# A Swin block on one core: plain float32 products in 128x32 tiles, a fourth strip of tokens moved by DMA, against split products

## The chip, the cores and the metric

The kernel runs on one core of one Trainium2 chip. The metric is the device time of one execution in microseconds (us).

## What is computed

The input x is float32 of shape (4, 96, 128, 128): 4 images, 96 channels. One Swin transformer block is followed by a generalised divisive normalisation. Cut to what matters:

```python
y = ln(x, norm1) ; roll by (-4, -4) ; cut into 8x8 windows of N = 64 tokens
qkv = y @ qkv_w.T + qkv_b              # 6 heads of 16 channels
attn = softmax(q @ k.T * 16 ** -0.5 + mask)
out = (attn @ v) @ proj_w.T + proj_b   # windows put back, rolled by (4, 4)
x2 = x + out
h1 = gelu(ln(x2, norm2) @ w1.T + b1)   # 384 hidden channels
x3 = x2 + h1 @ w2.T + b2
result = x3 * rsqrt(gamma @ x3**2 + beta)   # over the 96 channels
```

## The kernel before, in words

**Halves and rounds.** A unit is one row of 16 windows (1024 tokens); there are 64 units, and each is worked in two halves of 512 tokens, so 128 halves. The program is a software pipeline: in round H each engine runs its stages, every stage on half H plus its offset. The offsets stand in one line of constants: TURN_IN 4, TURN_OUT 3, QK 1, ATTEND 0, PROJECT -1, MLP -2, SETTLE -3, DIVIDE -4. The order in which an engine takes its stages is written out by hand in a function `steps`, one for each engine, and every engine works strictly in that order. In the last rounds a hand-written list (`late`) takes the place of the loop.

**Layouts.** Products have channels on 96 partitions and 512 tokens in the free dimension. The sums of probabilities and the product with v (lines 1081 to 1094) already use tiles of 128 rows and 32 columns of the array: three head pairs go to partitions 0 to 95, for 384 tokens each, and the fourth strip of partitions (96 to 127) takes the other 128 tokens of all three, so that four tiles work together. The division (lines 831 and 833) brings that strip back to the three head pairs in three short instructions.

**Products in parts.** q, k, the way up and down of the MLP and the denominators run as three float32r products each (`in_parts`, line 999: high times high, low times high, high times low). The parts of the activations are made by GpSimd (`split_hi`, `split_lo`, lines 452 and 457), those of the MLP's input y2 by VectorE (`split_y2`). The projection (line 1105) is one plain float32 product. v (line 1032) is 32 small plain products.

**Keys.** k goes from PSUM to SBUF by ScalarE (`k_copy`, line 577), and SyncE's queue (SP) then copies it by six DMAs, one for each head, into the block-diagonal `k_block` (`copy_keys`, line 378). `scores` (line 1058) waits for them. SP also loads x (two DMAs for a unit, line 350) and stores the output (two DMAs for a unit, line 387). SP issues in order: a DMA whose wait is not met holds back those behind it.

**Banks.** Two PSUM banks serve nearly all products in turn (`MM_ITEMS`); a product waits until the product two places before it has been read out. ScalarE loads a table twice a round (line 539), once for gelu and once for exp and ln.

## Time and profile before

| | |
|---|---|
| median of 3 runs | 1768.49 us (1768.0 to 1774.17) |
| span of the profiled execution | 1766.9 us |
| around the span: median less span | 1.6 us |
| busy: TensorE, VectorE, ScalarE, GpSimd | 97%, 92%, 86%, 77% |
| chain that ended last | 96% on TensorE |
| DMA | mean 46 GB/s, 81.35 MB |

The times shown are those of whole executions; the span is from the first to the last instruction of one profiled execution, whose own time is not listed apart. Busy shares are of the span. Register, semaphore and DMA-issuing instructions are not counted as busy, so SyncE has no share there; its issues are seen in the timeline and by line.

### The profile page before, as it was taken

Reading aid. Unit: us, or ns where it says so; the run is one execution under the profiler, and the core shown is the slowest. Engines: PE = TensorE matmul, PEld = TensorE weight load, DVE = VectorE, ACT = ScalarE, POOL = GpSimd, SP = SyncE. Lnnn points to the kernel's source line nnn. Section 1 sums busy time; section 2 is a strip of 40 time slices with the busy share of each in tenths; the row PEclk is TensorE's granted clock in tenths of the full one; section 3 lists DMA queues with packets and bytes.
Section 4 is the critical chain, followed back from the end, with each engine's and each line's share of the span. In section 5 each row is a group of like instructions: output and inputs, shape, how many; then the busy total and the mean of one; then the engine's idle time right before and its main releaser. Section 6 shows DMA issues by size and latency. Waiting matters only on the chain.

```text
span 1766.9 us, 81406 instructions
## 1 busy us (share of the span) xinstructions
PE 1720.2 (97%) x32612; PEld 1252.8 (71%) x32612; DVE 1629.6 (92%) x4508; ACT 1527.5 (86%) x2832; POOL 1356.5 (77%) x1532
## 2 busy tenths in 40 slices
PE   4999999999999999999999999999999999999996
PEld 2677777777777777777777777777777777777763
DVE  5899999999999999999999999999999999999983
ACT  2798998988898988988898888998888898998986
POOL 3478878878878878878778877888878878878862
PEclk9999999999999999999999999999999999999997
DMA  2122122122122122122122122122122122122111
GB/s 58 27 46 52 37 54 52 37 54 53 37 53 52 36 54 52 38 53 52 36 55 52 36 55 50 37 56 52 35 56 49 37 56 51 37 55 52 28 32 27
DMA packets 215154, 81.35 MB, mean 46 GB/s; under 512 B 116118, under 2 KB 214780, under 8 KB 214780
## 3 DMA queue, kind: packets, MB, share of 16 engines
q1 hardware_dynamic: 214218, 76.04, 19.7%
q8 instruction: 261, 4.28, 1.0%
q14 instruction: 113, 0.93, 0.2%
q10 hardware_dynamic: 562, 0.11, 0.0%
HBM read 25.75 MB, written 25.17 MB: 29 GB/s over the span
## 4 chain that ended last, share of the span: by engine, by line
PE 96%; DVE 1%; issue 1%; ACT 1%; DMA 0%; SPq 0%; POOL 0%; POOLq 0%; DVEq 0%
PE mm_bank L999 49%; PE score_banks L1058 8%; PE score_banks L947 7%; PE mm_bank L1105 6%; PE mm_bank L1032 5%; PE pv_bank L1081 5%; PE turn_banks L939 5%; PE turn_banks L953 3%; PE mm_bank L1094 3%; PE mm_bank L1091 3%; PE score_banks L1066 1%; PE mm_bank L1134 0%; DMA x_ext<-in_x 0%; DVE stats L767 0%; SPq L378 0%
## 5 line engine op out<-in xcount | busy, mean ns | idle before, releaser
L457 POOL TENSOR_TENSOR hidden_lo<-hidden,hidden_hi 128x512 fp32r<-128x512 f32 x378 | 480.9, 1286 | 0.0
L618 ACT ACTIVATE hidden<-mm_bank 128x512 f32<-128x512 f32 x381 | 227.8, 598 | 124.1 <-PE mm_bank L999 111.8
L539 ACT ACT_TABLE_LOAD x253 | 324.6, 1283 | 4.5
L452 POOL TENSOR_SCALAR y_hi<-y 96x512 fp32r<-96x512 f32 x128 | 108.1, 845 | 206.8 <-ACT y L563 206.8
L812 DVE TENSOR_REDUCE row_max<-score_banks 128x8 f32<-128x512 f32 x384 | 250.8, 681 | 10.8 <-PE score_banks L1066 8.1
L820 DVE TENSOR_TENSOR shifted<-score_banks,row_max 128x512 f32<-128x512 f32 x384 | 250.7, 680 | 0.0
L469 POOL TENSOR_TENSOR x_sq<-x 96x512 f32<-96x512 f32 x126 | 130.8, 1038 | 152.2 <-DVE x L846 152.2
L585 ACT ACTIVATE probs<-shifted 128x512 f32<-128x512 f32 x384 | 236.2, 627 | 10.6 <-DVE shifted L820 3.4
L452 POOL TENSOR_SCALAR hidden_hi<-hidden 128x512 fp32r<-128x512 f32 x378 | 229.8, 619 | 1.3 <-ACT hidden L618 1.3
L597 ACT ACTIVATE probs_t<-score_banks 128x512 f32<-128x512 f32 x384 | 215.1, 602 | 0.0
L767 DVE BATCH_NORM_STATS2 stats<-turn_banks 128x6 f32<-128x96 f32 x1024 | 191.1, 248 | 17.1 <-PE turn_banks L939 17.1
L947 PEld LDWEIGHTS score_banks<-ident_sb,probs 64*128 64x128 f32 x3072 | 148.3, 139 | 53.9 <-ACT probs L585 28.2
L947 PE MATMUL score_banks<-ident_sb,probs 64*128 64x64 f32 x3072 | 184.3, 230 | 1.6 <-issue 1.1
L999 PE MATMUL mm_bank<-y_hi,w_hi 97*128 97x512 f32 x381 | 172.1, 452 | 1.0 <-ACT hidden L618 0.6
L457 POOL TENSOR_TENSOR y_lo<-y,y_hi 96x512 fp32r<-96x512 f32 x128 | 164.3, 1284 | 1.1 <-POOL y_hi L452 1.1
L457 POOL TENSOR_TENSOR x_sq_lo<-x_sq,x_sq_hi 96x512 fp32r<-96x512 f32 x126 | 160.9, 1277 | 0.7 <-POOL x_sq_hi L452 0.7
L999 PE MATMUL mm_bank<-hidden_hi,w_hi 128*96 128x512 f32 x378 | 160.6, 425 | 0.0
L776 DVE TENSOR_TENSOR turn_banks<-turn_banks,moments 128x384 f32<-128x384 f32 x256 | 145.0, 567 | 8.8
L1058 PE MATMUL score_banks<-k_block,q 32*64 32x128 f32 x6144 | 148.6, 275 | 3.9 <-DMA k_block<-k 2.5
L999 PE MATMUL mm_bank<-y_lo,w_hi 97*128 97x512 f32 x381 | 151.4, 397 | 0.0
L999 PE MATMUL mm_bank<-y_hi,w_lo 97*128 97x512 f32 x381 | 150.5, 395 | 0.0
L999 PE MATMUL mm_bank<-hidden_hi,w_lo 128*96 128x512 f32 x378 | 149.7, 396 | 0.0
(132 smaller groups left out, 4489.2 us busy)
## 6 DMA issues: line engine op xcount, KB each, us to landing
x_ext<-in_x SPq DMA_DIRECT2D x128, 192.0 KB, 2.9
k_block<-k SPq DMA_DIRECT2D x768, 32.0 KB
out<-o_ext SPq DMA_DIRECT2D x128, 192.0 KB, 2.6
w_raw<-in_w_t SPq DMA_DIRECT2D x1, 144.0 KB
w<-in_w_t SPq DMA_DIRECT2D x1, 144.0 KB
qkv_raw<-in_qkv_t ACTq DMA_DIRECT2D x1, 108.0 KB
ident_sb<-in_ident SPq DMA_DIRECT2D x1, 64.0 KB, 2.2
q_quadrants<-in_qmask SPq DMA_DIRECT2D x3, 1.0 KB
```

Source lines behind the costliest of these rows:

```text
L452: nc.gpsimd.tensor_scalar(hi, whole, 1.0, 1.0, ALU.mult, ALU.mult).then_inc(hi_ready, 1)
L457: nc.gpsimd.tensor_tensor(lo, whole, hi, ALU.subtract).then_inc(is_split, 1)
L539: nc.scalar.preload_act_table_set(name)
L585: nc.scalar.activation(probs[:, g, :, :, :].rearrange("t p j k -> t (p j k)"), shifted[:, g, :, :].rearrange("t i k -> t (i k)"), ACT.Exp)\
L597: nc.scalar.activation(dst, src, ACT.Copy).then_inc(probs_t_ready, 1)
L618: nc.scalar.activation(hidden_of(A)[:, n, :], up_bank(A, n), ACT.Gelu).then_inc(gelu_ready, 1)
L767: made = nc.vector.bn_stats(stats[ln][:, c, :], turn_banks[:, ln, n * DIM:(n + 1) * DIM])
L812: nc.vector.tensor_reduce(row_max[:, g, :], group_scores(g), op=ALU.max, axis=AX.X)\
L820: nc.vector.tensor_tensor(shifted[:, g, :, :], group_scores(g), row_max[:, g, :].unsqueeze(2) .broadcast_to([128, PAIRS * TILE_HEADS, TOKE ...
L947: return nc.tensor.transpose(score_banks[:, bank, first:first + TOKENS], probs[half, m, p, :, :], ident_sb[half, half])
L999: made = nc.tensor.matmul(out, w, x_part, start=first and part == 0, stop=last and part == 2)
L1058: made = nc.tensor.matmul(score_banks[64 * n:64 * n + 64, r, cols], q[rows, unit_slot(a), (w + n) * TOKENS:(w + n + 1) * TOKENS], k_block[ ...
```

## The change

- q, k, the projection, the way down and the denominators become plain float32 products in 128x32 tiles (`in_strips`): three matmuls of 384 tokens for the three groups of 32 output channels, and three of 128 tokens whose results all go to the fourth strip. The way up stays in three float32r parts. v becomes four matmuls with all 128 columns for the tokens of a pair of windows, written to `pv_bank` (no `mm_bank`); `v_blocks` then makes four copies in place of one masked product.
- In that layout q, attended, x2 and x3 hold the last (or first) 128 tokens on partitions 96 to 127. The residuals (`first_residual`, `second_residual`) and `outputs` work on 128 partitions and 384 columns. x is loaded with the strip beside it (five DMAs for a unit in place of two), and the output is stored by five. Where a product contracts over the channels, the strip has to come back to partitions 0 to 95: SP does this with three DMAs for q, three for attended and three for x3, for each half. The keys go in 12 DMAs (six windows from partitions 0 to 95, two from the strip, for each head) in place of six.
- GpSimd no longer splits anything. It squares x3 and adds the biases of the projection and of the MLP to x and x2 (`bias_x`, `bias_x2`). The projection and MLP biases leave the matrices.
- The mean of the layer norms is taken out through the weights (their column sums, at the start), so the centring of the tokens and the aggregation instructions go, and four small VectorE instructions a round (`variances`) give the variance.
- The pipeline is deeper: PROJECT -2, MLP -3 (now only the turning of y2), UP -4 (the way up), SETTLE -5, DIVIDE -6. The hand-written end goes; the loop runs on for seven rounds. q comes right after k; the projection and the way down come ahead of the transposes of probabilities; v, now behind them.

The core of the diff (the renaming of arguments and the declarations are left out):

```diff
-X_SLOTS = 4
+X_SLOTS = 5
+Y_SLOTS = 3
+X2_SLOTS = 4
+KEY_COPIES = 2 * HEADS
+IMAGE_MOVES = 5
 QKV_CONSTS = 6
-MLP_CONSTS = 9
-MLP_WEIGHTS = 3
-
-TURN_IN, TURN_OUT, QK, ATTEND, PROJECT, MLP, SETTLE, DIVIDE = 4, 3, 1, 0, -1, -2, -3, -4
+MLP_CONSTS = 19
+FOLDS = 17
+
+TURN_IN, TURN_OUT, QK, ATTEND, PROJECT, MLP, UP, SETTLE, DIVIDE = 4, 3, 1, 0, -2, -3, -4, -5, -6
 
...
         MM_ITEMS = [
             ("k", QK, k_ready, 1, 1),
+            ("q", QK, q_ready, 1, 1),
             ("den", DIVIDE, log_den_made, 1, 1),
             ("sum", ATTEND - 1, log_sum_made, 1, 1),
-            ("v", ATTEND, v_ready, 1, 1),
-            ("q", QK, q_ready, 1, 1),
+            ("proj", PROJECT, x2_ready, 1, 1),
             ("mlp2", SETTLE, x3_ready, 1, 1),
-            ("proj", PROJECT, x2_ready, 1, 1),
-            ("mlp1_0", MLP, gelu_ready, HID_CHUNKS, 1),
-            ("mlp1_1", MLP, gelu_ready, HID_CHUNKS, 2),
-            ("mlp1_2", MLP, gelu_ready, HID_CHUNKS, 3),
+            ("mlp1_0", UP, gelu_ready, HID_CHUNKS, 1),
+            ("mlp1_1", UP, gelu_ready, HID_CHUNKS, 2),
+            ("mlp1_2", UP, gelu_ready, HID_CHUNKS, 3),
         ]
-        FINAL = HALVES - 1
-        MM_FINISH = [
-            ("sum", FINAL), ("den", FINAL - 3), ("proj", FINAL), ("mlp2", FINAL - 2),
-            ("mlp1_0", FINAL - 1), ("mlp1_1", FINAL - 1), ("mlp1_2", FINAL - 1), ("den", FINAL - 2),
-            ("mlp2", FINAL - 1), ("mlp2", FINAL), ("den", FINAL - 1), ("den", FINAL),
-        ]
-        MM_ORDER = [(item[0], H + item[1]) for H in range(-TURN_IN - 1, HALVES) for item in MM_ITEMS
-                    if has(H + item[1])] + MM_FINISH
+        MM_ORDER = [(item[0], H + item[1]) for H in range(FIRST_ROUND, END_ROUND) for item in MM_ITEMS
+                    if has(H + item[1])]
...
+            def load_x(A):
...
+                    first = image_rows(unit)[0][1]
+                    for j in range(HEAD_PAIRS):
+                        sp.dma_start(x_ext[strip, slot, 2 + 2 * j:4 + 2 * j, 0:WIDTH],
+                                     x[bass.ds(unit // ROWS, 1), group(j), bass.ds(first, 2), :]
+                                     .rearrange("n c h w -> (n c) h w")).then_inc(x_loaded[slot], 16)
...
+            def copy_keys(A):
 
...
+                first, last = (A % 2) * HALF_WINDOWS, (A % 2 + 1) * HALF_WINDOWS
                 for head in range(HEADS):
                     rows = slice(HEAD_DIM * head, HEAD_DIM * (head + 1))
...
-                    sp.dma_start(k_block[rows, half_windows(a), head % TILE_HEADS, :],
-                                 half_of(k, a)[rows, :].rearrange("c (n t) -> c n t", t=TOKENS))\
-                        .then_inc(keys_copied[a % 2], 16)
...
+                    sp.dma_start(k_block[rows, first:last - 2, head % TILE_HEADS, :],
+                                 k[rows, A % 2, :].rearrange("c (n t) -> c n t", t=TOKENS))\
+                        .then_inc(keys_copied[A % 2], 16)
+                for head in range(HEADS):
+                    rows = slice(HEAD_DIM * head, HEAD_DIM * (head + 1))
+                    at = DIM + HEAD_DIM * (head % TILE_HEADS)
+                    sp.dma_start(k_block[rows, last - 2:last, head % TILE_HEADS, :],
+                                 k[at:at + HEAD_DIM, A % 2, group(head // TILE_HEADS, 128)]
+                                 .rearrange("c (n t) -> c n t", t=TOKENS)).then_inc(keys_copied[A % 2], 16)
+
+            def move_queries(A):
+
+                wait_alone(sp, q_ready, A + 1)
+                for j in range(HEAD_PAIRS):
+                    sp.dma_start(q[group(j), A % 2, MAIN:HALF], q[strip, A % 2, group(j, 128)])\
+                        .then_inc(q_moved[A % 2], 16)
+
+            def move_attended(A):
+
+                wait_alone(sp, attended_ready, A + 1)
+                for j in range(HEAD_PAIRS):
+                    sp.dma_start(attended[group(j), MAIN:HALF], attended[strip, group(j, 128)])\
+                        .then_inc(attended_moved, 16)
+
+            def move_x3(A):
+
+                wait_alone(sp, x3_ready, A + 1)
+                for j in range(HEAD_PAIRS):
+                    sp.dma_start(x3[group(j), A % 2, MAIN:HALF], x3[strip, A % 2, group(j, 128)])\
+                        .then_inc(x3_moved[A % 2], 16)
+
...
+                    stores = [(to[:, bass.ds(first + 2, 2), :], o_ext[0:DIM, slot, 2:4, 0:WIDTH]),
+                              (to[:, bass.ds(second, SHIFT), :], o_ext[0:DIM, slot, 4:8, 0:WIDTH])]
+                    stores += [(to[group(j), bass.ds(first, 2), :],
+                                o_ext[strip, slot, 2 + 2 * j:4 + 2 * j, 0:WIDTH]) for j in range(HEAD_PAIRS)]
+                    for dst, src in stores:
+                        sp.dma_start(dst, src).then_inc(out_stored[slot], 16)
...
-                run(store_out, DIVIDE - 1)
+                run(move_queries, QK)
+                run(move_attended, ATTEND - 1)
+                run(move_x3, SETTLE)
+                run(store_out, DIVIDE)
...
+            def bias_x(A):
+
+                if A % 2 == 1:
+                    if A == 1:
+                        wait_alone(pool, mlp_loaded, 16 * MLP_CONSTS)
+                    wait_alone(pool, x_turned[0], A + 1)
+                    rows = x_ext[:, unit_slot(A, X_SLOTS), 2:WIN, :].rearrange("c (j i) w -> c j (i w)", i=2)
+                    width = 2 * (WIDTH + SHIFT)
+                    nc.gpsimd.tensor_tensor(rows, rows, proj_bias[:, :].unsqueeze(2)
+                                            .broadcast_to([128, HEAD_PAIRS, width]), ALU.add).then_inc(x_biased, 2)
+
+            def bias_x2(A):
+
+                wait_alone(pool, x_turned[1], A + 1)
+                tokens = by_group(x2[:, A % X2_SLOTS, :])
+                nc.gpsimd.tensor_tensor(tokens, tokens, b2_bias[:, :].unsqueeze(2)
+                                        .broadcast_to([128, HEAD_PAIRS, 128]), ALU.add).then_inc(x2_biased, 1)
+
...
+            def divide(A):
                 dve.wait_ge(inv_sum_ready, A + 1)
                 dve.wait_ge(pv_made, A + 1)
                 wait(dve, proj_made, A)
-                for m in range(HEAD_PAIRS):
-                    cols = slice(m * 2 * TOKENS, (m + 1) * 2 * TOKENS)
-                    nc.vector.tensor_tensor(attended[32 * m:32 * m + 32, MAIN:HALF], pv_bank[DIM:128, cols],
-                                            inv_sum[DIM:128, cols], ALU.mult)
-                nc.vector.tensor_tensor(attended[0:DIM, 0:MAIN], pv_bank[0:DIM, 0:MAIN],
-                                        inv_sum[0:DIM, :], ALU.mult).then_inc(attended_ready, 1)
-
-            def first_residual(A, a):
+                nc.vector.tensor_tensor(attended[:, 0:MAIN], pv_bank[:, 0:MAIN], inv_sum[:, :],
...
+            def in_strips(to, weights, main, last):
+
+                for j in range(HEAD_PAIRS):
+                    nc.tensor.matmul(to[group(j), 0:MAIN], weights[:, group(j)], main, start=True, stop=True)
+                for j in range(HEAD_PAIRS):
+                    made = nc.tensor.matmul(to[strip, group(j, 128)], weights[:, group(j)], last,
+                                            start=True, stop=True)
+                return made
+
...
+            def project_v(A):
+
+                wait(pe, attended_ready, A)
+                for p in range(PAIRS):
+                    made = nc.tensor.matmul(pv_bank[:, p * DIM:(p + 1) * DIM], y1_windows(A, 2 * p, 2 * p + 2),
+                                            wv[:, :], start=True, stop=True)
                 made.then_inc(v_made, 1)
...
+                pe.wait_ge(gelu_ready, HID_CHUNKS * (A + 1))
                 mm_wait("mlp2", A)
+                to = mm_bank("mlp2", A)
                 for n in range(HID_CHUNKS):
-                    pe.wait_ge(gelu_ready, HID_CHUNKS * A + n + 1)
-                    made = nc.tensor.matmul(mm_bank("mlp2", A)[0:DIM, :], w2[:, n, :], hidden_of(A)[:, n, :],
-                                            start=n == 0, stop=n == HID_CHUNKS - 1)
+                    first, last = n == 0, n == HID_CHUNKS - 1
+                    for j in range(HEAD_PAIRS):
+                        nc.tensor.matmul(to[group(j), 0:MAIN], w2[:, n, group(j)], hidden[:, n, 128:HALF],
+                                         start=first, stop=last)
+                    for c in range(HID_CHUNKS):
+                        made = nc.tensor.matmul(to[strip, group(n, 128)], w2[:, c, group(n)],
+                                                hidden[:, c, 0:128], start=c == 0, stop=c == HID_CHUNKS - 1)
                 made.then_inc(mlp2_made, 1)
...
-            def denominators(A, a):
-                pe.wait_ge(sq_split, A + 1)
-                mm_wait("den", A)
-                in_parts(mm_bank("den", A)[0:DIM, :], wgdn_hi[:, :], wgdn_lo[:, :],
-                         x3_sq_hi[:, :], x3_sq_lo[:, :]).then_inc(den_made, 1)
+                in_strips(mm_bank("den", A), wgdn, x3_sq[:, 0:MAIN], x3_sq[:, MAIN:HALF]).then_inc(den_made, 1)
 
             def steps(run, H):
 
                 run(scores, ATTEND)
                 run(project_k, QK)
+                run(project_q, QK)
                 run(denominators, DIVIDE)
                 run(sum_probs, ATTEND - 1)
                 run(times_v, ATTEND - 1)
+                run(project, PROJECT)
+                run(mlp_down, SETTLE)
+                turn_run(H)
                 run(project_v, ATTEND)
-                run(project_q, QK)
-                turn_run(H)
-                for n in range(HID_CHUNKS):
-                    run(mlp_down, SETTLE, n)
-                run(project, PROJECT)
+                run(mlp_up, UP, 0)
                 run(turn_in, TURN_IN, 0)
                 if H == -TURN_IN:
```

On SP two rounds in the middle of the program, of before. The rows give the line of the kernel, the destination and source and the destination's shape:

```order
L350 DMA x_ext<-in_x 96x4x128 [waits x2_ready]
L350 DMA x_ext<-in_x 96x4x128
L378 DMA k_block<-k 16x8x64 [waits k_ready,scores_made]
L378 DMA k_block<-k 16x8x64 x5
L378 DMA k_block<-k 16x8x64 [waits k_ready,scores_made]
L378 DMA k_block<-k 16x8x64 x5
L387 DMA out<-o_ext 96x4x128 [waits out_wrapped]
L387 DMA out<-o_ext 96x4x128
```

And one round of the change, the one with a store, with the start of the next:

```order
L362 DMA k_block<-k 16x6x64 [waits k_ready,scores_made]
L362 DMA k_block<-k 16x6x64 x5
L368 DMA k_block<-k 16x2x64 x6
L376 DMA q<-q 32x128 [waits q_ready]
L376 DMA q<-q 32x128 x2
L383 DMA attended<-attended 32x128 [waits attended_ready]
L383 DMA attended<-attended 32x128 x2
L390 DMA x<-x 32x128 [waits x3_ready]
L390 DMA x<-x 32x128 x2
L404 DMA out<-o_ext 96x2x128 [waits out_wrapped]
L404 DMA out<-o_ext 96x4x128
L404 DMA out<-o_ext 32x2x128 x3
```

In two rounds SP has 16 DMAs before and 52 now; a round always holds 21, and a load or a store of five comes in every second one each.

On TensorE, from the scores to the transposes of the probabilities, of before:

```order
L1058 MATMUL score_banks<-k_block,q 64x128 x24
L1066 MATMUL score_banks<-k_masks,q_quadrants 64x128 x3
L999 MATMUL mm_bank<-y_hi,wk_hi 96x512
L999 MATMUL mm_bank<-y_hi,wk_lo 96x512
L999 MATMUL mm_bank<-y_lo,wk_hi 96x512
L999 MATMUL mm_bank<-x_sq_hi,wgdn_hi 96x512
L999 MATMUL mm_bank<-x_sq_hi,wgdn_lo 96x512
L999 MATMUL mm_bank<-x_sq_lo,wgdn_hi 96x512
L1091 MATMUL mm_bank<-probs_t,ones_pair_sb 32x384 x3
L1094 MATMUL mm_bank<-probs_t,ones_pair_sb 32x128 x3
L1081 MATMUL pv_bank<-probs_t,v_block 32x64 x24
L1032 MATMUL mm_bank<-wv,y 32x48 x32
```

And of the change:

```order
L1030 MATMUL score_banks<-k_block,q 64x128 x24
L903 MATMUL mm_bank<-y,wk 32x384 x3
L905 MATMUL mm_bank<-y,wk 32x128 x3
L903 MATMUL mm_bank<-y,wq 32x384 x3
L905 MATMUL mm_bank<-y,wq 32x128 x3
L903 MATMUL mm_bank<-x_sq,wgdn 32x384 x3
L905 MATMUL mm_bank<-x_sq,wgdn 32x128 x3
L1062 MATMUL mm_bank<-probs_t,ones_pair_sb 32x384 x3
L1065 MATMUL mm_bank<-probs_t,ones_pair_sb 32x128 x3
L1051 MATMUL pv_bank<-probs_t,v_block 32x64 x24
L903 MATMUL mm_bank<-attended,wproj 32x384 x3
L905 MATMUL mm_bank<-attended,wproj 32x128 x3
```

q has moved ahead of the denominators, and from k to the way down everything is one shape of tile.

## Rows read from the trace of the kernel before

**Rows 1.** The page, parts 1 and 4: TensorE's busy time; the chain by engine.

```profile
PE 1720.2 (97%) x32612; PEld 1252.8 (71%) x32612; DVE 1629.6 (92%) x4508; ACT 1527.5 (86%) x2832; POOL 1356.5 (77%) x1532
...
PE 96%; DVE 1%; issue 1%; ACT 1%; DMA 0%; SPq 0%; POOL 0%; POOLq 0%; DVEq 0%
```

**Rows 2.** The waits of SP's queue: waited for, us in total, times, longest.

```profile
SPq L241 <- ACT k L577: 799.4, 128, 15.6
SPq L241 <- DVE x L838: 150.9, 60, 5.2
SPq L241 <- POOL o_ext L498: 59.3, 22, 24.7
```

**Rows 3.** SP's issues by line: duration ns min/median/max, first and last start us.

```profile
L378 SPq DMA_DIRECT2D k_block<-k x768: 585/601/1867, 26.7 to 1706.7; - x192
...
L350 SPq DMA_DIRECT2D x_ext<-in_x x128: 319/474/1903, 1.2 to 1631.3; - x128
```

**Rows 4.** Timeline of SP, first 12 us: start us, us, line, out<-in xcount.

```profile
3.06 0.32 SPq L402 DMA_DIRECT2D gdn_raw<-in_gamma_t  x1
...
5.01 0.42 SPq L402 DMA_DIRECT2D ones_pair_sb<-in_ones_pair  x1
5.48 0.43 SPq L402 DMA_DIRECT2D wproj<-in_proj_t  x1
```

**Rows 5.** Timeline of SP, 803 to 817 us, in short windows.

```profile
803.11 0.60 SPq L378 DMA_DIRECT2D k_block<-k  x1
...
803.84 2.25 SPq L387 DMA_DIRECT2D out<-o_ext  x2
...
812.45 1.24 SPq L378 DMA_DIRECT2D k_block<-k  x2
...
813.73 1.37 SPq L378 DMA_DIRECT2D k_block<-k  x1
...
816.43 0.60 SPq L378 DMA_DIRECT2D k_block<-k  x1
```

**Rows 6.** The page, part 6: a DMA's median time from issue to landing, last.

```profile
x_ext<-in_x SPq DMA_DIRECT2D x128, 192.0 KB, 2.9
```

**Rows 7.** Timeline of TensorE, one round: start us, us until the last ends.

```profile
803.50 0.48 PE L999 MATMUL mm_bank<-hidden_hi,w_hi 128*96 128x512 f32 x1
...
805.67 1.02 PE L1105 MATMUL mm_bank<-attended,wproj 97*96 97x512 f32 x2
806.53 0.50 PE L939 MATMUL turn_banks<-ident_sb,x_ext 96*128 96x96 f32 x4
...
810.70 0.47 PE L999 MATMUL mm_bank<-y_hi,wk_hi 97*96 97x512 f32 x1
...
811.49 0.39 PE L999 MATMUL mm_bank<-x_sq_hi,wgdn_hi 97*96 97x512 f32 x1
...
812.34 0.52 PE L1091 MATMUL mm_bank<-probs_t,ones_pair_sb 128*32 128x384 f32 x3
...
813.01 0.86 PE L1081 MATMUL pv_bank<-probs_t,v_block 128*32 128x64 f32 x48
813.68 0.88 PE L1032 MATMUL mm_bank<-wv,y 97*32 97x48 f32 x64
814.48 0.48 PE L999 MATMUL mm_bank<-y_hi,wq_hi 97*96 97x512 f32 x1
```

**Rows 8.** Timeline of ScalarE around the exponential table's load.

```profile
808.86 1.28 ACT L618 ACTIVATE hidden<-mm_bank 128x512 f32<-128x512 f32 x2
810.16 1.28 ACT L539 ACT_TABLE_LOAD   x1
811.69 0.59 ACT L577 ACTIVATE k<-mm_bank 96x512 f32<-96x512 f32 x1 [0.25 <-PE mm_bank L999]
```

**Rows 9.** The last stretch: us, PE, PEld, DVE, ACT, POOL busy, PEclk, DMA share, GB/s.

```profile
1740.00:1767.00 27.00, 16.21 (x51) 8.54 (x50) 9.13 (x20) 11.97 (x18) 3.80 (x5) 0.82 0.11 29
```

**Rows 10.** Groups of VectorE's instructions by line: busy us, mean ns, idle before.

```profile
L776 DVE TENSOR_TENSOR turn_banks<-turn_banks,moments 128x384 f32<-128x384 f32 x256 | 145.0, 567 | 8.8
```

778 lines of the change are left out of this document (334 added, 444 removed).

## The prediction

> **What bounds the kernel now.** I read the page first: TensorE is busy for 1720.2 of 1766.9 us and the chain that ended last lies on it for 96% [rows 1]. So today a round lasts as long as TensorE's work in it. The first key copy is issued at 26.7 us and the last at 1706.7 [rows 3]; 127 rounds lie between, 13.2 us each. Ahead of them are 27 us, behind them 60.
>
> The change takes work from TensorE, VectorE and GpSimd and adds DMAs, all on SP. So the next view is the one on SP's queue. It waits 799.4 us for k, 150.9 us for x2 and 59.3 us for the output, 1010 us in all [rows 2]. The other 757 us are issuing: 5.9 us a round for 8 DMAs. The reader is to see in [rows 3, 5] that an issue isn't free: a key copy holds SP for at least 585 ns and 601 at the median; two follow each other 0.64 us apart; and six of them, 812.45 to 817.03, take 4.58 us because one took 1.37. The order of SP before and after says what is added: 52 DMAs in two rounds in place of 16, 18 more a round.
>
> **The change on SP.** What does an added issue cost? The trace shows three kinds.
> - The second six key copies have the kind of the first (SBUF to SBUF, 16 partitions, windows apart): 0.64 us each, 3.8 a round [rows 5].
> - The nine moves of strips (32 partitions, 512 bytes each, SBUF to SBUF) have no row of their own. By shape they are nearest to the weight loads, which follow each other 0.47 us apart (5.01 to 5.48) [rows 4]; by place, both ends in SBUF, to the key copies at 0.64. I take the middle, 0.56: 5.0 a round. The ends kept for the range are 0.36 (the shortest load, 319 ns [rows 3], with a gap of 0.04) and 0.76 (the mean in the burst with the long issue).
> - Three more loads or stores a round, the loads' median 474 ns [rows 3], with the gap 0.52: 1.6.
> - Three more waits on semaphores: after the last key copy (803.11 plus 0.60) the store is issued 0.13 later, 0.09 more than between two copies [rows 5]: 0.3 a round.
>
> Sum: 5.9 + 3.8 + 5.0 + 1.6 + 0.3 = **16.6 us a round on SP**, against 13.2 for a whole round today. The cover is gone: SP had 7.3 us idle a round, and 10.7 are added. Put the other way, the round stays at 13.2 only if the 18 added issues cost (13.2 - 5.9 - 0.3) / 18 = 0.39 us each; every row that follows another issue is above that, only issues after an idle queue are below. With all 18 at 0.36 SP needs 12.7, with 15 at 0.47 it is 14.8, with 15 at 0.76 it is 19.2.
>
> Does SP really work without a break then? The waits in front of it: with q of the next half issued at time T, its landing is about 2 us later (a DMA takes 2.9 from issue to landing, issue included [rows 6]), scores 0.94, k 0.67, its copy 0.6: k of the half after is ready at T + 4.3. SP meanwhile issues attended, x3 and on average 5 loads and stores, 6.2 us. attended and x3 belong to halves whose products began a round before. So every wait of SP is met when it comes to it, and its sum is the round.
>
> **The change on the engines**, hidden by that. TensorE: between the rows of one round [rows 7] k takes 0.79 us, the denominators 0.85, the way down 2.17, the projection 0.86, v 0.80, and the sums of probabilities, the very form that the change gives to all, 0.67. q, k, denominators and projection at 0.67 and the way down at 3 x 0.65 save 0.12 + 0.15 + 0.18 + 0.19 + 0.22 = 0.86. v as four matmuls lies between 0.28 (four transposes of 96 columns, 806.53 to the next product) and 0.80; I take 0.70. So 13.26 becomes about 12.3 and, masks counted only every second round, 12.1. But the order has a new wait: the denominators use the bank of k and the sums that of q. k can be copied only behind two gelus and the table load [rows 8], and q behind k and the two short rstd instructions, about 3.5 us after the scores' start, when TensorE would be at the sums after 2.95. That gives back 0.5 or more: **12.8**.
> VectorE loses the centring (145.0 us [rows 10]), the aggregation, the three short divisions and a fourth of the residuals' and outputs' columns, and gains four small instructions and copies of v in place of a product: well under its 1630 us [rows 1], no bound. ScalarE keeps both table loads and drops a quarter of the columns of k, q and the denominators: less than its 1528, so below 11.9 a round. GpSimd loses all splitting, most of its 1357 us, and gains two additions. All this lies beside SP's queue and is worth nothing while that decides.
>
> At 812.34 the sums begin 0.15 later than the preceding products' pace would let them [rows 7], at a change of tile shape. The Trainium skill ("TensorEngine Tiling (Array Packing)", Key Properties) says that changing the tiling mode drains the engine; the new order has two such changes fewer a round, so by it TensorE would need some 0.2 us less, which moves the engines' 12.8 and not SP's 16.6.
>
> **Sum.** 27 us to the first key copy, 127 rounds of 16.6 (2108), less 12 because the first six rounds have no x3 to move, and an end of 65: seven rounds run on, one full at 12.8, the others with little but the MLP, two table loads of 1.28 and three gelus, near 7 each; today's hand-made end takes 60. 27 + 2108 - 12 + 65 = 2188 in the profile's time; the median of runs is 1.6 above the span shown, so **2190 us**.
>
> **Rivals.**
> 1. *SP's issues are cheap and the engines decide: faster.* If a two-dimensional or small copy holds SP for no more than 0.32 to 0.33 us, as the shortest load does [rows 3], SP's sum falls to 12.7 and the round is the 12.8 of the engines: 27 + 127 x 12.8 + 65 = 1718, **1720 us**. The point from which it decides is 0.37 us an added issue. For it: the spare time on all engines, and a weight load of 0.32 [rows 4]. Against it: 768 key copies with none below 585 ns. The Trainium skill ("SBUF — State Buffer", The DMA setup-cost knee) makes nearly all of a DMA's fixed 2 us completion latency and puts sequencer and generator at about 50 ns plus a few hundred. At 250 ns, an estimate from that page, SP would need 10.7 us a round and this rival would hold; the key copies' rows do not agree with it.
> 2. *The loop through the keys.* Moves cheap, keys not: then SP's sum can fall below the loop from scores to the next scores: 0.94 + 0.67 + 0.6 for k, 12 keys of 0.64 (7.7), the wait and two issues of q (1.2), 2.9 from the last issue to landing: 14.0. 27 + 127 x 14.0 + 55 is about **1860 us**. For it speaks that scores now wait for q's move, issued behind twelve keys; it decides once SP's sum is below 14.0.
> 3. *The clock falls.* TensorE would be idle 4 us in each round, ahead of the scores. In the last 27 us, where it is busy for 16.21, its granted clock is 0.82, a mixture of 2.4 and 1.2 GHz [rows 9]. A third of each round at 1.2 GHz would fit in the 16.6; the whole of it would be about 24 us a round and over 3000 us. Its price starts only beyond the idle time.
>
> **How the numbers follow.** SP's queue as the bound has 0.71, the loop 0.09, the clock 0.04, the engines 0.16. The first three are slower; of the last I give 0.02 to an outcome near 1768, where the added issues are about 0.39. A measurement tells about 0.5% from no change. So faster 0.14, same 0.03, slower 0.83. The range takes in the loop and, of SP's sums, 13.9 to 18.6 us a round: 1840 to 2440 us. It leaves out the engines' case and 0.04 above.
>
> **What would show it.** In the profile after: SP waiting for almost nothing; key copies still near 600 ns, moves 0.45 to 0.6; TensorE near 70 to 75% busy, its idle time ahead of the scores and ended by the moves of q or the keys; the products in tiles 0.67 us apart; VectorE under 1500 us busy; a round of 16 to 17 us. I'm wrong if moves of strips issue in 0.35 us or less, if SP still waits hundreds of us for k, or if TensorE's longest idle time is ended by ScalarE's copies.

## The result, and the profile after

The change takes **2375.59 us** (median of 4 runs, 2366.15 to 2380.48) against 1771.33 us for the kernel before on the same chip: ratio 1.3403, 95% interval 1.3365 to 1.3442. The profiled execution has a span of 2375.1 us and a mean granted clock of 0.875 on TensorE.

The page of the kernel after, parts 1, 2 (TensorE's clock) and 4, beside [rows 1]:

```profile
PE 1927.0 (81%) x33524; PEld 1643.2 (69%) x33524; DVE 1397.8 (59%) x3886; ACT 1473.8 (62%) x2829; POOL 355.6 (15%) x459
...
PEclk9799889989889888888898888889898898889888
...
SPq 86%; issue 8%; PE 3%; DMA 1%; ACT 0%; DVE 0%; POOL 0%; POOLq 0%; DVEq 0%
SPq L362 22%; SPq L368 22%; SPq L390 11%; SPq L376 9%; SPq L383 9%; SPq L404 6%; SPq L334 4%; SPq L329 3%; PE mm_bank L905 1%; PE score_banks L1030 1%; DMA q<-q 1%; SPq L238 1%; DMA x<-x 1%; PE mm_bank L1101 0%; PE mm_bank L903 0%
```

The chain that ended last lay on TensorE for 96%; now it lies on SP's queue for 86%, and the key copies (L362, L368) and the moves of strips (L376, L383, L390) are its largest parts. No engine is busy for more than 81%.

The waits of SP's queue after, for which [rows 2] stand before:

```profile
SPq L238 <- ACT k L565: 25.8, 9, 5.7
SPq L238 <- DVE x L825: 24.7, 4, 8.5
SPq L238 <- DVE attended L809: 12.6, 2, 8.3
SPq L238 <- POOL o_ext L493: 6.2, 1, 6.2
```

1010 us of waiting have become 69, and of these only 2.4 lie between 200 and 2290 us: there SP issues without a break.

SP's issues by line after (duration ns min/median/max, first and last start us), for [rows 3]:

```profile
L362 SPq DMA_DIRECT2D k_block<-k x768: 589/602/1991, 24.6 to 2292.8; - x192
...
L368 SPq DMA_DIRECT2D k_block<-k x768: 585/593/1831, 28.6 to 2297.1; - x192
...
L376 SPq DMA_DIRECT2D q<-q x384: 542/590/1753, 32.5 to 2299.0; - x192
...
L383 SPq DMA_DIRECT2D attended<-attended x384: 507/590/1921, 66.7 to 2324.8; - x192
...
L390 SPq DMA_DIRECT2D x<-x x384: 507/590/1934, 134.1 to 2364.1; - x192
...
L404 SPq DMA_DIRECT2D out<-o_ext x320: 322/451/2093, 170.6 to 2372.8; - x160
```

The moves have their own rows now: 590 ns at the median, as dear as the key copies, though each of them moves one piece of 512 bytes a partition. An issue with an end in DRAM (L404) takes 451. From L362's first start to its last, 127 rounds take 2268.2 us: **17.86 us a round**, where [rows 3] gave 13.2.

One round of SP's timeline after (start us, us, line, count), and the moves of q and x3 of the next, for [rows 5]:

```profile
1144.01 3.88 SPq L362 DMA_DIRECT2D k_block<-k  x6
1147.94 4.32 SPq L368 DMA_DIRECT2D k_block<-k  x6
1152.38 1.83 SPq L376 DMA_DIRECT2D q<-q  x3
1154.33 1.79 SPq L383 DMA_DIRECT2D attended<-attended  x3
1156.23 1.78 SPq L390 DMA_DIRECT2D x<-x  x3
1158.13 1.03 SPq L329 DMA_DIRECT2D x_ext<-in_x  x2
1159.21 2.38 SPq L334 DMA_DIRECT2D x_ext<-in_x  x3
...
1170.60 1.83 SPq L376 DMA_DIRECT2D q<-q  x3
...
1174.43 2.72 SPq L390 DMA_DIRECT2D x<-x  x3
```

The next round begins at 1161.77. Nothing lies between the issues of two lines but 0.05 to 0.18 us. Six copies take 3.88, or 4.32 where one of them is long; the nine moves with their waits take 5.75 (1152.38 to 1158.13); the three loads of L334 take 2.38, and if two of them took the median of 0.43, one took 1.44.

The scores shown next wait for the moves of q issued from 1170.60 on, the denominators behind them for the moves of x3 issued from 1174.43 on. TensorE's timeline after, 1173 to 1180 us, for [rows 7]:

```profile
1173.92 1.85 PE L1030 MATMUL score_banks<-k_block,q 32*64 32x128 f32 x48 [2.01 <-DMA q<-q]
1175.71 0.86 PE L903 MATMUL mm_bank<-y,wk 97*32 97x384 f32 x3
...
1176.99 0.86 PE L903 MATMUL mm_bank<-y,wq 97*32 97x384 f32 x3
...
1179.72 0.86 PE L903 MATMUL mm_bank<-x_sq,wgdn 97*32 97x384 f32 x3 [1.23 <-POOL x_sq L485]
```

and its waits over the whole span (us in total, times, longest), with GpSimd's own wait behind the first of them:

```profile
POOL x_sq L485 <- DMA x<-x: 1478.2, 128, 24.5
...
PE mm_bank L903 <- POOL x_sq L485: 270.3, 119, 5.1
PE score_banks L1030 <- DMA q<-q: 114.4, 62, 8.1
```

TensorE waits in two places: ahead of the scores for q's moves, in 62 rounds, and longer ahead of the denominators, in 119 rounds, for the squares, which GpSimd can make only when the moves of x3, the last of SP's moves in a round, have landed. Both waits end with SP's queue.

The clock. The windows of the round from 1160 us (us, PE, PEld, DVE, ACT, POOL busy, PEclk, DMA share, GB/s):

```profile
1160.00:1172.00 12.00, 11.56 (x207) 9.82 (x199) 9.66 (x25) 9.54 (x21) 1.52 (x3) 1.00 0.23 52
1172.00:1177.50 5.50, 3.58 (x66) 3.02 (x70) 2.62 (x10) 2.01 (x3) 0.00 (x0) 0.70 0.10 25
```

TensorE was idle for 2.01 us up to 1173.92, and the second window, which holds that idle time, has a granted clock of 0.70, a mixture of the two levels (2.4 and 1.2 GHz). k takes 1.28 here (1175.71 to 1176.99) and the scores 1.79; in a round at the full clock (from 1210 us) they take 0.67 and 1.05. That lies beside SP's issuing; b_more18 below shows how far the clock is a consequence.

### The profile page after: what moved, and what is told of

It reads as the page before. It is cut to its first block, busy times and chain, and to the rows that moved or that the text cites. A ratio compares the mean times of both kernels' runs of the same rounds, so it can differ in the third digit from the quotient of the medians.

```text
span 2375.1 us, 84051 instructions
## 1 busy us (share of the span) xinstructions
PE 1927.0 (81%) x33524; PEld 1643.2 (69%) x33524; DVE 1397.8 (59%) x3886; ACT 1473.8 (62%) x2829; POOL 355.6 (15%) x459
## 4 chain that ended last, share of the span: by engine, by line
SPq 86%; issue 8%; PE 3%; DMA 1%; ACT 0%; DVE 0%; POOL 0%; POOLq 0%; DVEq 0%
SPq L362 22%; SPq L368 22%; SPq L390 11%; SPq L376 9%; SPq L383 9%; SPq L404 6%; SPq L334 4%; SPq L329 3%; PE mm_bank L905 1%; PE score_banks L1030 1%; DMA q<-q 1%; SPq L238 1%; DMA x<-x 1%; PE mm_bank L1101 0%; PE mm_bank L903 0%
## 5 line engine op out<-in xcount | busy, mean ns | idle before, releaser
L903 PE MATMUL mm_bank<-x_sq,wgdn 97*32 97x384 f32 x768 | 158.3, 706 | 270.8 <-POOL x_sq L485 270.3
L816 DVE TENSOR_TENSOR x<-mm_bank,x_ext 128x384 f32<-128x384 f32 x128 | 71.3, 557 | 420.5 <-PE mm_bank L905 420.5
L1101 PE MATMUL mm_bank<-hidden,w 128*32 128x128 f32 x2304 | 286.9, 281 | 0.0
L1098 PE MATMUL mm_bank<-hidden,w 128*32 128x384 f32 x2304 | 285.3, 507 | 0.1
L1101 PEld LDWEIGHTS mm_bank<-hidden,w 128*32 128x32 f32 x2304 | 263.5, 115 | 5.1
L1030 PE MATMUL score_banks<-k_block,q 32*64 32x128 f32 x6144 | 168.5, 300 | 115.9 <-DMA q<-q 114.4
L1030 PEld LDWEIGHTS score_banks<-k_block,q 32*64 32x64 f32 x6144 | 132.4, 146 | 164.3 <-issue 164.3
L771 DVE TENSOR_TENSOR y_lo<-turn_banks,y_hi 96x512 fp32r<-96x512 f32 x128 | 87.9, 687 | 194.2 <-ACT y L547 191.2
L553 ACT ACTIVATE y_hi<-turn_banks 96x512 fp32r<-96x512 f32 x128 | 76.0, 593 | 202.7 <-PE turn_banks L941 202.7
L784 DVE COPY v_block<-pv_bank 64x192 f32<-64x192 f32 x512 | 180.6, 353 | 12.3 <-PE pv_bank L1005 7.1
L1051 PEld LDWEIGHTS pv_bank<-probs_t,v_block 128*32 128x32 f32 x6144 | 180.8, 155 | 5.7
```

What stands on the lines that cost most here:

```text
L1030: made = nc.tensor.matmul(score_banks[64 * n:64 * n + 64, r, cols], q[rows, A % 2, (2 * p + n) * TOKENS:(2 * p + n + 1) * TOKENS], k_block ...
L1098: nc.tensor.matmul(to[group(j), 0:MAIN], w2[:, n, group(j)], hidden[:, n, 128:HALF], start=first, stop=last)
L1101: made = nc.tensor.matmul(to[strip, group(n, 128)], w2[:, c, group(n)], hidden[:, c, 0:128], start=c == 0, stop=c == HID_CHUNKS - 1)
```

## The experiments

A round is here the time from the first to the last matmul of the scores, divided by 127. The third column is the kernel before on the same chip in the same series. Where "one run" stands, the kernel ran once, and there is no interval.

| kernel | us | before | ratio, 95% interval | round, us |
|---|---|---|---|---|
| before | 1771.33 | | | 13.2 |
| after | 2375.59 | 1771.33 | 1.3403 (1.3365 to 1.3442) | 17.9 |
| b_more9 | 1783.79 | 1769.02 | one run | 13.4 |
| b_more18 | 2415.09 | 1769.02 | one run | 18.3 |
| a_noq | 2142.76 | 1769.02 | one run | 16.0 |
| a_pool | 1878.42 | 1769.02 | 1.0603 (1.0552 to 1.0653) | 13.9 |
| b_tiny18 | 2153.97 | 1774.70 | one run | 16.3 |
| a_tiny3 | 2609.25 | 1774.70 | one run | 19.7 |
| a_nomoves | 1802.59 | 1774.70 | 1.0171 (1.0138 to 1.0203) | 13.5 |
| a_pool2 | 1857.36 | 1774.70 | 1.0489 (1.0447 to 1.0532) | 13.8 |
| b_load18 | 1769.35 | 1773.85 | one run | 13.2 |
| a_nomoves_up | 1762.36 | 1773.85 | 0.9951 (0.9928 to 0.9975) | 13.2 |
| a_pool3 | 1860.74 | 1773.85 | 1.0520 (1.0470 to 1.0571) | 13.8 |
| a_pool4 | 1822.73 | 1769.43 | 1.0291 (1.0266 to 1.0317) | 13.5 |

**b_more9 and b_more18: the kernel before, with SP's added issues alone.** Nothing of the change is in them but 9 or 18 more DMAs a round on SP, each of 16 KB between two SBUF tiles. The edit is shown with 18; b_more9 has 9 in its place.

```diff
+            def spare_moves(A, a):
+                if A > 1:
+                    wait_alone(sp, spare_moved[A % 2], 16 * 18 * (A // 2))
...
+                for n in range(18):
+                    sp.dma_start(spare[32 * (n % 3):32 * (n % 3) + 32, A % 2, n // 3, :], ident_sb[96:128, :])\
+                        .then_inc(spare_moved[A % 2], 16)
...
                 run(copy_keys, QK)
+                run(spare_moves, QK)
```

> The kernel before, with nine more copies a round on SP (32 partitions of 512 bytes, from the identity matrix to a spare tile; the result does not use them). Theory (SP's issues set the change's round): SP then needs 5.9 + 9 x 0.66 + 0.1 = 11.9 us a round, under the 13.2 of TensorE, so the time stays within 1% of 1770 us. Rival (more DMAs slow the others by traffic or by landing later): slower by several per cent already here.

> The kernel before, with eighteen more such copies a round, as many DMAs as the change adds, and nothing else of the change. Theory: SP needs 5.9 + 18 x 0.66 + 0.1 = 17.9 us a round, above 13.2, so 127 x 17.9 + 90 = 2360 us, the change's own time. Rival (the new products, their new waits for ScalarE and the fallen clock make the change slow): about 1770 us, or a small loss.

With nine, 1783.79 us: SP still waits 185 us, and the round is nearly unchanged. With eighteen, 2415.09 us, 40 us more than the change itself and 55 more than expected: 227 of the 2304 added issues took over 0.9 us, and their mean was 0.67. SP's waits in b_more18:

```profile
SPq L243 <- POOL o_ext L513: 35.4, 3, 23.7
SPq L243 <- ACT k L592: 15.7, 1, 15.7
```

Between nine and eighteen SP's idle time of 7.3 us a round is used up, and from there each issue lengthens the round. The clock comes out at 0.864 in b_more18, where TensorE's products are those of the kernel before: so the low clock needs nothing of the new tiles; that TensorE is made to wait is enough.

**a_noq: the change with three of the moves fewer.** The part of q that they would bring is zero, so these scores are left out.

```diff
-                run(move_queries, QK)
...
-                wait_alone(pe, q_moved[A % 2], 16 * HEAD_PAIRS * (A // 2 + 1))
```

> The change without the three moves of q a round; that part of q is set to zero once, so the scores of the last two windows of each half are left out of the computation. Theory: three issues of 0.66 us and a wait of 0.1 go from SP's round of 17.9: 15.8, 2375 - 128 x 2.1 = 2107 us. Rival (engines or clock set the round): within 2% of 2375 us. Rival (the landing of q ahead of the scores is what costs, 114 us of TensorE's waits): 2260 us.

2142.76 us, 36 above what was expected and far from both rivals. Three issues and a wait less are 233 us less, 1.83 a round, 0.61 for each, which is what the three take in SP's timeline (1.83). So these issues were on the path with their whole length. With them gone SP's queue is still 68% of the chain and waits 85 us.

**a_tiny3: the change with three more DMAs of 4 bytes.** The edit is `spare_moves` with 3 and the shape of b_tiny18 below.

> The change with three more DMAs a round on SP, each of 4 bytes in one partition. Theory: with SP full, even tiny issues lengthen the round: 3 x 0.34 + 0.1 = 1.1 us, 2375 + 128 x 1.1 = 2516 us. Rival (bytes, landings or engines set the round): within 1% of 2375 us.

2609.25 us, 234 more for 384 DMAs of 4 bytes, 0.61 each. The expectation was 93 too low: it counted on issues 0.34 apart, and these took 598 ns at the median. The mean clock falls further, to 0.829.

**b_tiny18 and b_load18: what makes an issue dear.** First the 18 added DMAs with 4 bytes in place of 16 KB, both ends in SBUF:

```diff
+                    sp.dma_start(spare[n:n + 1, A % 2, 0, 0:1], ident_sb[96:97, 0:1])\
```

> The kernel before with eighteen more DMAs a round on SP, each of 4 bytes in one partition. Theory (the time that an issue holds SP is what counts): an issue of one partition took 0.25 to 0.33 us at the start, so SP needs 5.9 + 18 x 0.34 + 0.1 = 12.1 us a round, under 13.2: 1770 to 1800 us. Rival (the number of DMAs or of their landings counts, whatever their size): about 2400 us, as with the eighteen larger copies.

2153.97 us, neither the one nor the other. Size matters little between SBUF and SBUF: an issue took 543 ns with 4 bytes here, and 598 in a_tiny3, where those of the moves take 590. What the small ones lack is long issues: none of the 2304 took over 0.70 us. So the next run kept the 4 bytes and changed where they come from, DRAM instead of SBUF:

```diff
-                    sp.dma_start(spare[n:n + 1, A % 2, 0, 0:1], ident_sb[96:97, 0:1])\
+                    sp.dma_start(spare[n:n + 1, A % 2, 0, 0:1], ident[96:97, 0:1])\
```

> The kernel before with 18 more DMAs of 4 bytes a round on SP, as in b_tiny18, but each with its source in DRAM (a constant of the inputs) in place of SBUF. Theory (an issue is dear when both ends are in SBUF, whatever its size): with a DRAM end an issue takes 0.28 to 0.33 us (the shortest load of the kernel before takes 319 ns), apart 0.33; SP needs 5.9 + 0.1 + 18 x 0.33 = 11.9 us a round, below 13.2, so the time stays within 1.5% of the kernel before (1775 to 1800). Rival (every further issue costs near 0.59, whatever its ends, because SP issues faster than the rings drain): 16.5 us a round again and about 2150 us.

1769.35 us, level with the kernel before. The 18 issues by line (duration ns min/median/max) and in SP's timeline (start us, us), first of b_tiny18:

```profile
L391 SPq DMA_DIRECT2D spare<-ident_sb x2304: 542/543/697, 30.6 to 2105.4; - x192
```
```profile
1004.66 10.68 SPq L391 DMA_DIRECT2D spare<-ident_sb  x18
```

and the same two views of b_load18:

```profile
L391 SPq DMA_DIRECT2D spare<-in_ident x2304: 220/252/448, 30.7 to 1712.2; - x192
```
```profile
1005.47 5.73 SPq L391 DMA_DIRECT2D spare<-in_ident  x18
```

The same 4 bytes cost SP 0.59 us an issue from SBUF to SBUF and 0.32 from DRAM to SBUF. The number of DMAs and of landings is the same in both, so they are not what costs. For 4 bytes the source decides the price. For larger DMAs with an end in DRAM it doesn't alone: the loads and stores of this kernel take 427 to 510 ns at the median. The moves of this change have the dear kind. The Trainium skill ("SBUF — State Buffer", The DMA setup-cost knee) puts sequencer and generator at about 50 ns and a few hundred: the row of b_load18, 252 ns, agrees; that of b_tiny18, 543, is about twice the row of b_load18. Why, no run here tells.

**a_nomoves: what would be left if SP had nothing to move.** The nine moves and the waits for them are gone, and what they would bring of q, attended and x3 is a constant, so these tokens are left out. SP keeps the keys, the loads and the stores.

```diff
-                run(move_queries, QK)
-                run(move_attended, ATTEND - 1)
-                run(move_x3, SETTLE)
...
-                wait_alone(pe, q_moved[A % 2], 16 * HEAD_PAIRS * (A // 2 + 1))
...
-                pe.wait_ge(attended_moved, 16 * HEAD_PAIRS * (A + 1))
...
-                wait_alone(pool, x3_moved[A % 2], 16 * HEAD_PAIRS * (A // 2 + 1))
```

> The change without any of the nine moves and without the waits for them; the strips' last columns of q, attended and x3 are constants, so these tokens are left out of the computation. It measures the engines' round of the change. Forecast of the prediction: 12.8 us a round, 1720 us. Rival (the engines have not gained, 13.2 us a round or more, because v in four matmuls takes 0.9 us and the way up now waits for y2's low part, both seen in the run with moves on GpSimd): 1770 to 1800 us. Rival (the landing of moves played no part and the clock or TensorE itself is the bound): above 1850 us.

1802.59 us, 1.7% above the kernel before. Even with SP out of the way the engines' side of the change is not faster. TensorE's timeline of a_nomoves shows a place where it stands:

```profile
1000.91 1.13 PE L1005 MATMUL pv_bank<-wv,y 97*128 97x96 f32 x8
1001.83 0.47 PE L1085 MATMUL mm_bank<-y_hi,w_hi 97*128 97x512 f32 x1
...
1003.06 0.52 PE L922 MATMUL turn_banks<-ident_sb,x_ext 96*128 96x96 f32 x4 [0.30 <-DVE y_lo L771]
```

v takes 0.92 us (1000.91 to 1001.83), against 0.80 for the 32 small matmuls in [rows 7]. Ahead of the turning of x TensorE waits for y2's low part to be read out of the bank, 121 times, 35.8 us in all. And from the second half of q to the denominators it is 0.60 (1007.66 to 1008.26), where half a product takes 0.32. By the order of the banks this is the wait for the one that k's copy frees; no row names it.

**a_nomoves_up: that wait covered.** a_nomoves, and on TensorE:

```diff
                 run(mlp_up, UP, 0)
+                run(mlp_up, UP, 1)
                 run(turn_in, TURN_IN, 0)
...
                 run(turn_in, PROJECT, 1)
-                run(mlp_up, UP, 1)
                 run(mlp_up, UP, 2)
```

> a_nomoves (the change without its nine moves, so its output lacks what the moved strips carry) with the second chunk of the way up moved ahead of the turning of x. Theory (TensorE waits 0.3 us a round for y2's low part ahead of the turning, and this is what keeps the engines' round of the change at 13.47): the 0.7 us of the way up cover that wait, the round falls to 13.2 and the time from 1803 to about 1770, level with the kernel before. Rival (the wait only moves, to the scores, that wait for the keys 0.3 us later anyway, or to the third chunk that waits for its bank): 1795 to 1805.

1762.36 us (8 runs, 1757.2 to 1770.98), 0.5% below the kernel before and 40 us below a_nomoves. The wait is gone from TensorE's timeline:

```profile
1010.28 0.39 PE L1085 MATMUL mm_bank<-y_lo,w_hi 97*128 97x512 f32 x1
1010.51 0.49 PE L922 MATMUL turn_banks<-ident_sb,x_ext 96*128 96x96 f32 x4
```

This is the best that the engines' side of the change gave in these runs, the moves left out: a round of 13.17 in place of 13.24. It isn't quite the engines alone: SP's queue, with 12 key copies a round, is 17% of the chain, and TensorE waits 31.3 us, in 35 rounds, for key copies.

**a_pool, a_pool2, a_pool3, a_pool4: the whole change, its moves issued elsewhere.** GpSimd is idle for 85% of the change, so in a_pool it issues the nine moves:

```diff
-                run(move_queries, QK)
-                run(move_attended, ATTEND - 1)
-                run(move_x3, SETTLE)
                 run(store_out, DIVIDE)
...
+                run(move_queries, QK)
                 run(wrap_out, DIVIDE)
+                run(move_attended, ATTEND - 1)
+                run(move_x3, SETTLE)
                 run(square, SETTLE)
```

> The change with the nine moves of q, attended and x3 issued by GpSimd, which is busy 15% of the time, in place of SP. Theory: SP is left with 12 keys and 5 loads and stores, 11.7 us a round, so the engines' round decides: 12.8 us forecast, 1720 us, if GpSimd can issue nine DMAs in under 9 us. Rival (the DMAs themselves, their landing or the engines are the bound): within 3% of 2375 us. Between them if GpSimd needs over a microsecond for each issue: its 2.8 us of work and 9 issues then are the round.

1878.42 us. Most of the loss is back, 497 of 604 us, by moving nine issues from one queue to another. An issue costs GpSimd 498 ns at the median. The rest of the expected gain was held by waits that the expectation hadn't counted: TensorE's waits in a_pool (us in total, times, longest),

```profile
PE turn_banks L922 <- DVE y_lo L771: 35.6, 121, 1.0
PE mm_bank L903 <- POOL x_sq L461: 32.3, 20, 5.2
PE mm_bank L1062 <- ACT q L559: 26.5, 16, 2.0
PE score_banks L1030 <- DMA k_block<-k: 25.6, 18, 5.9
```

and behind the second of them GpSimd's square, which waits 258.7 us for the moves of x3 just ahead of it in its own queue. a_pool2 puts the moves of x3 first and q's copy ahead of the rstd instructions:

```diff
                 run(move_queries, QK)
-                run(wrap_out, DIVIDE)
-                run(move_attended, ATTEND - 1)
                 run(move_x3, SETTLE)
+                run(move_attended, ATTEND - 1)
                 run(square, SETTLE)
+                run(wrap_out, DIVIDE)
...
-                rstd_pair(H)
                 run(q_copy, QK)
+                rstd_pair(H)
```

> The change with the nine moves on GpSimd as before, there x3's moves first and the output's wrap behind the square, and on ScalarE the copy of q ahead of the two rstd instructions. In the run with moves on GpSimd TensorE waited 77 us for the squares and 27 us and more for the copy of q. If these waits are what the round has over the engines' own, 1878 - 100 = 1780 us; if the engines alone set it, still 1850 or more.

1857.36 us: 21 us better, 77 above what was expected. The expectation had added TensorE's wait for the squares (32.3 us) and that of its weight loads (45.1 us), which lie beside each other. The scores' wait for the keys had grown to 36.9 us. a_pool3 is a_pool2 with the reordering of a_nomoves_up:

> a_pool2 (the whole change, with its nine moves issued by GpSimd, nothing left out) with the same reordering as a_nomoves_up. Theory: 0.3 us a round less, 1857 falls to about 1820, still above the kernel before, since the keys' 12 issues on SP stay on the loop from k to the scores. Rival: if that loop decides in most rounds, nothing is gained, 1850 to 1860. If everything the engines can give shows, 1770.

1860.74 us, the rival's case: what the reordering had given a_nomoves (40 us) shows nowhere here. TensorE's wait ahead of the scores in a_pool3:

```profile
PE score_banks L1030 <- DMA k_block<-k: 63.2, 70, 4.7
```

Each time one wait went, the keys' wait grew: 25.6, 36.9, 63.2 us. The edit of a_pool2 has a part in that. With the output's wrap behind the square, SP now waits for the wrap at every store, and the keys of the next half stand behind the store. SP's waits and timeline in a_pool3:

```profile
SPq L238 <- POOL o_ext L490: 185.8, 64, 18.5
```
```profile
1000.51 3.12 SPq L383 DMA_DIRECT2D out<-o_ext  x5
1003.82 3.80 SPq L362 DMA_DIRECT2D k_block<-k  x6
```

k was copied out at 1002.72 there, 1.1 us before its first copy was issued. In a_pool SP waited for the wrap 5 times, 65.4 us, and for k in all 128 rounds; in a_pool3 it waits for k in 73. Over the rounds 8 to 119 of a_pool3, the scores wait 31 us for keys issued behind a store and 12 us for those behind a load. The order without this wait (moves of x3 first, the wrap where it was) was not run.

a_pool4 takes six of the twelve key copies off SP and puts them on GpSimd behind q's moves:

```diff
-                for head in range(HEADS):
...
-                    sp.dma_start(k_block[rows, last - 2:last, head % TILE_HEADS, :],
...
+            def copy_strip_keys(A):
...
+                    pool.dma_start(k_block[rows, last - 2:last, head % TILE_HEADS, :],
...
                 run(move_queries, QK)
+                run(copy_strip_keys, QK)
```

> a_pool3 (the whole change, its nine moves issued by GpSimd, the second chunk of the way up ahead of the turning of x) with the six key copies that come from the strip issued by GpSimd too, behind q's moves, where its queue stands idle some 4 us a round. Nothing is left out. SP keeps 6 key copies, the loads and the stores: some 6.5 us a round. Theory (in a_pool3 the loop from k through SP's twelve key issues of 0.64 to the next scores sets the round, which took back what a_nomoves_up had shown the engines to give): the keys are issued in 4 us in place of 7.7, the loop falls to about 11 us, and the round to the engines' 13.2: 1762 of a_nomoves_up plus a longer start, 1765 to 1780, within 0.5% of the kernel before. Rival (the DMAs of both queues delay each other, or GpSimd's issue work and its waits in order delay the moves of x3 and the squares): 1820 to 1860.

1822.73 us (5 runs, 1820.67 to 1826.98), the best whole version of the change, and still 2.9% slower than the kernel before. The keys' wait is nearly gone. Since SP issues only six copies behind a store now, this run doesn't tell the twelve issues from the delay by the store. TensorE's waits in a_pool4 begin with

```profile
PE mm_bank L1110 <- ACT log_sum L599: 47.1, 64, 1.0
...
PE score_banks L1042 <- DMA k_block<-k: 6.8, 5, 3.2
```

What took its place lies in part between GpSimd and VectorE: VectorE is 23% of the chain that ended last, 5% with one small instruction (L746), where it has 0% in a_nomoves_up. GpSimd's timeline in a_pool4:

```profile
1002.79 1.50 POOL L442 TENSOR_TENSOR x_ext<-x_ext,proj_bias 128x792 f32<-128x792 f32 x1
1005.65 1.03 POOL L477 DMA_DIRECT2D q<-q  x2 [1.36 <-ACT q L569]
1009.07 0.50 POOL L477 DMA_DIRECT2D q<-q  x1 [2.39 <-issue]
```

and VectorE's, behind it the group of its first instruction over the whole span (count, busy us, mean ns, idle before):

```profile
1002.71 1.61 DVE L746 TENSOR_TENSOR mean_gap<-stats 128x8 f32<-128x8 f32 x1
```
```profile
L746 DVE TENSOR_TENSOR mean_gap<-stats 128x8 f32<-128x8 f32 x122 | 122.8, 1007 | 13.0 <-DVE stats L733 0.5
```

An instruction of 8 columns on VectorE takes 1.61 us and ends at 1004.32, when GpSimd's addition ends (1004.29). Its mean is 1007 ns in a_pool4, 893 in a_pool3 and 551 in a_nomoves_up, and VectorE's busy time in a_pool4 1525.7 us against 1420.6 in a_nomoves_up. The Trainium skill ("SBUF — State Buffer", SBUF: two separate sides) says that a VectorE instruction with two SBUF inputs and a GpSimd instruction that reads SBUF lock each other out of a shared pair of ports. This instruction has two SBUF inputs (both parts of `stats`), the addition reads SBUF, and the two rows end within 0.03 us of each other, which agrees. GpSimd's third issue of q's moves starts 2.39 us late with nothing in the profile to wait for. That VectorE held it too was not tried, and how the 60 us between a_pool4 and a_nomoves_up divide stays open.

## Why the prediction was right, and where it was off

**The bound.** The forecast was that SP's queue becomes the bound and the engines' work is hidden beside it, 2190 us; 2375.59 was measured, inside the range of 1840 to 2440 and on the side that had 0.83. SP's waits fell from 1010 to 69 us, the chain has SP at 86%, and b_more18 gives the same loss without any of the change's products. The mechanism is shown, from both sides: issues alone bring the loss, and moving nine of them takes 497 of 604 us back.

**The term that was off: SP's sum.** It was 16.6 us a round and was 17.86, 1.3 too small.

- *The moves, 0.56 an issue.* They stand 0.59 to 0.61 apart (three in 1.78 to 1.83). The working had laid them between the weight loads at 0.47 and the key copies at 0.64, by shape and by place. b_tiny18 shows that place was the better guide: with both ends in SBUF even 4 bytes take 0.59. 0.61 for nine is 0.5 a round more.
- *No long issues among the added ones.* The 5.9 of the old issues was a mean over the program and held its long issues; the added ones were priced at medians (0.64, 0.56, 0.52). But issues up to 2 us come among all of them: in the round shown one of L334 took 1.44 for 0.43, and L368's six took 4.32 for 3.8. The two are 1.5 us in that round. Over the whole program the durations of SP's issues exceed the medians of their lines by 195 us after and by 93 us before, which the 5.9 held: 0.8 a round more, and that is what is left of the difference. [rows 5] showed such a burst, at 0.76 an issue; it was kept for the range and left out of the sum.
- *The end, 65 us.* From the start of the last of L362's issues to the end it is 82.3 (2292.8 to 2375.1).

The three account for the difference. 127 rounds of 17.86 against 16.6 are 160 us more; the 12 us taken off for the first six rounds are in the measured mean already and come back: 172. The end is 17 more, the start (24.6 for 27) 2 less: 2188 + 187 = 2375.

**A row read wrongly.** The prediction says that every issue that follows another stands more than 0.39 us behind it, and that only issues after an idle queue are cheaper. Before's timeline of SP, just behind the 3.06 of [rows 4], has

```profile
3.42 0.28 SPq L402 DMA_DIRECT2D gdn_raw<-in_beta  x1
3.75 0.25 SPq L402 DMA_DIRECT2D wproj<-in_proj_b  x1
```

0.36 and 0.33 apart, in an unbroken row of issues. These are small loads from DRAM, the kind that b_load18 found at 0.32. The rows gave no such case with both ends in SBUF, so the conclusion for the moves held, but not by the reason given.

**Where TensorE waits.** Forecast: ahead of the scores, for q's moves or the keys. q's moves are there, with 114.4 us; but the longer wait, 270.3, is at the denominators. In SP's order the moves of x3 come last of the moves in a round, and the square and the denominators stand behind them. The text had looked at what SP waits for and not at who waits for SP's last issues. Its busy share is 81%, above the 70 to 75 of the forecast, since the same matmuls take longer at the lower clock (1927.0 us of busy time, for 1704.2 in a_nomoves).

**VectorE** under 1500 us: 1397.8. **Key copies** near 600 ns: 602 and 593. **Moves** 0.45 to 0.6: 0.59.

**The engines' 12.8.** Hidden by SP, and wrong. a_nomoves has 13.47. Two terms failed: v at 0.70, which takes 0.92, 0.12 more than before in place of 0.10 less; and the wait for y2's low part ahead of the turning of x, which the working did not have, 0.3 a round, as a_nomoves_up shows by covering it (13.17). Together they bring 12.8 to 13.3; the rest, under 0.2, stays open, and no run separates what the fewer changes of tile shape are worth. The products in tiles were right: k and q 0.64 to 0.67, the way down 6 by 0.32.

**The rivals.** *The engines decide* would have given 1720 us. Its condition (an added issue under 0.37 us) held only for 4 bytes from DRAM, at 0.32. Had it held for all, the engines give 1762 to 1803 and not 1720: a gain of half a per cent at best. So the rival's time was out of reach for a second reason, which the prediction didn't name. *The loop through the keys* is not what bounds the change. It gains weight once the moves are off SP: the keys' wait grows from 25.6 us in a_pool to 63.2 in a_pool3, and taking six issues out of the loop (a_pool4) brought 38 us. That the rounds of a_pool to a_pool3 (13.8 to 13.9) stand near the 14.0 of the forecast doesn't confirm it: in a_pool TensorE has 59% of the chain and SP 6%, and in a_pool3 part of the wait comes from the store. *The clock*: 0.875 on the mean. It fell, as [rows 9] let one expect, once TensorE was idle for a part of each round, but SP's issuing covers it: b_more18, with other products and nearly the same clock of 0.864, has nearly the same time, and in both SP waits for almost nothing (69 and 51 us).

## What to carry to other kernels

A queue that issues DMAs is an engine with a busy time of its own, though the page gives it no share: count its issues in a round, price each kind by its mean with the long ones in it, and compare the sum with the round before anything is moved onto it. Price a kind by a row with the same two ends before one with the same shape: here 4 bytes between SBUF and SBUF cost nearly as much as 16 KB. Then ask of the last issue in the queue's round who waits for it, since that place can be where the engines stand longest. And when work is put later in one queue, look for what waits for it in another: the wrap put behind the square held SP's store, and the keys with it. And before a product is cheapened at the price of moves, measure the change with the moves left out: here that gives half a per cent at best, and no whole version with the moves beat the kernel before.

## What the runs showed of the hardware

- On SP an issue from SBUF to SBUF took 0.54 to 0.60 us at the median, whatever its size (4 bytes: 543 ns in b_tiny18 and 598 in a_tiny3; 16 KB over 32 partitions: 590; 24 KB over 16 partitions: 602), one from DRAM to SBUF 252 ns for 4 bytes. The loads and stores of this kernel lie between (medians of 427 to 510 ns).
- Single issues of 1.0 to 2.1 us come among all the kernel's own kinds on SP, 254 of the change's 3328 above 0.9 us. Among the 4-byte DMAs of b_tiny18, b_load18 and a_tiny3 there is none above 0.70 us.
- An issue by GpSimd took 498 ns at the median for the same moves, and none over 0.67 us in a_pool.
- A VectorE instruction of 8 columns lasted until a GpSimd addition beside it ended, 1.61 us.
